# Attention on one core: the weights of four steps summed in two buffers, one of them in the place of four residual tiles

## The reference

```python
q, k = rope(q), rope(k)                     # each 16 x 2048 x 32
scores = q @ k.T / sqrt(32), causal
attn = softmax(scores)                      # over the keys
y = attn @ v
x = x + y.reshape(2048, 512) @ w_o
x = x + moe(rmsnorm(x, g2))
```

## Time and profile before

| | us |
|---|---|
| median of the runs | 2267.21 (2264.42 to 2269.95, 3 runs) |
| profiled execution, own time | 2257.79 |
| profiled execution, span | 2256.0 |
| attention stage in it | from about 965 to about 1709 |
| quad 1, from its first values to those of quad 2 | 1183.32 to 1341.37 |
| PE busy in the whole | 2048.9 (91%) |
| DVE, ACT, POOL busy | 1564.4, 1078.8, 581.5 |

### The profile page before, as it was taken

One profiled execution on the slowest core, in us unless ns is written; L12 is line 12 of the kernel. 1 busy time (PEld: TensorE's weight loads), 2 busy tenths in 40 slices (PEclk: granted clock), 3 DMA queues, 4 the chain that ended last, 5 costly groups with the idle time before them and its releaser, 6 DMA issues. The chain is left out here.

```text
span 2256.0 us, 42226 instructions
## 1 busy us (share of the span) xinstructions
PE 2048.9 (91%) x17716; PEld 1208.6 (54%) x17716; DVE 1564.4 (69%) x2563; ACT 1078.8 (48%) x1060; POOL 581.5 (26%) x447
## 2 busy tenths in 40 slices
PE   6899999999995899989999999999991599999997
PEld 3554444444442444544444444444440599999997
DVE  7789999999985666758777778778357544444442
ACT  6688898988980323213444444444330223332331
POOL 3410000000002012223454555545330222222211
PEclk9999999999998999959999999999995699999999
DMA  7321221212215013333013031010212444444421
GB/s 279 135 84 50 75 69 53 78 50 70 74 34 199 28 47 115 125 97 89 20 40 74 20 83 30 20 38 15 75 44 111 159 122 121 122 122 122 119 64 24
DMA packets 90905, 185.87 MB, mean 82 GB/s; under 512 B 14332, under 2 KB 23548, under 8 KB 86332
## 3 DMA queue, kind: packets, MB, share of 16 engines
q1 hardware_dynamic: 81756, 162.20, 22.0%
q0 software_dynamic: 8960, 20.98, 5.0%
HBM read 138.47 MB, written 40.23 MB: 79 GB/s over the span
## 5 line engine op out<-in xcount | busy, mean ns | idle before, releaser
L1515 DVE TENSOR_REDUCE t_rm<-t_m 128x1 f32<-128x512 f32 (+3 forms) x640 | 372.9, 606 | 148.5 <-PE t_m L1664 94.8
L1449 ACT ACTIVATE t_E<-t_s 128x1024 f32<-128x1024 f32 (+3 forms) x320 | 277.4, 895 | 410.9 <-PE t_s L1681 222.5
L1411 POOL TENSOR_TENSOR t_total<-t_E 128x1024 f32<-128x1024 f32 (+2 forms) x151 | 292.3, 1947 | 219.9 <-PE t_d L1708 214.1
L615 ACT ACTIVATE m_step<-m_ub,gat_bias 128x2048 bf16<-128x2048 f32 x128 | 250.0, 1989 | 13.9 <-DMA m_ub<-scratch_uac 8.5
L757 PE MATMUL m_bd<-m_mask,m_S 128*32 128x512 bf16 x3072 | 230.3, 379 | 11.0 <-DVE m_mask L705 11.0
L757 PE MATMUL m_bd<-gat_adjT,m_S 128*32 128x512 bf16 x2496 | 201.4, 379 | 4.8 <-PE m_dn L757 4.8
L757 PE MATMUL m_bd<-m_mask,m_neg 128*32 128x512 bf16 x2496 | 189.0, 379 | 0.0
L2038 POOL DMA_INDIRECT out<-e_ye,e_token x40 | 81.0, 2024 | 338.8 <-DVE e_ye L2141 334.1
L2202 PE MATMUL e_h<-e_xTh,e_w1h 128*128 128x320 f32 x512 | 159.0, 310 | 1.4 <-DVE e_xTl L2122 1.4
L2202 PE MATMUL e_h<-e_xTl,e_w1h 128*128 128x320 f32 x512 | 158.8, 310 | 0.0
L2202 PE MATMUL e_h<-e_xTh,e_w1l 128*128 128x320 f32 x512 | 158.8, 310 | 0.0
(11 more groups left out here) (362 smaller groups left out, 4084.6 us busy)
## 6 DMA issues: line engine op xcount, KB each, us to landing
a_adj<-in_adj SPq DMA_DIRECT2D x16, 1024.0 KB, 4.9
m_ub<-scratch_uac SPq DMA_DIRECT2D x16, 1024.0 KB, 5.1
e_w1r<-in_L_ffn_w SPq DMA_DIRECT2D x8, 2048.0 KB
e_w2r<-in_L_ffn_w SPq DMA_DIRECT2D x8, 2048.0 KB, 9.2
tq_Q<-scratch_parts SPq DMA_DIRECT2D x36, 256.0 KB, 4.6
gat_scale<-scratch_uac SPq DMA_DIRECT2D x32, 256.0 KB
scratch_parts<-o_hi SPq DMA_DIRECT2D x32, 256.0 KB, 2.2
scratch_parts<-o_lo SPq DMA_DIRECT2D x32, 256.0 KB, 2.7
```

Of the source, the lines that this page charges most:

```text
L615: act.activation(step(n), ub[h % 2][:, :].rearrange("p (t q) -> p t q", t=T), ACT.Relu, bias=bias[:, j, h:h + 1], scale=BIG).then_inc(step ...
L1411: pool.tensor_tensor(total[:, two, off:BANK], E[a % 3][:, two, off:BANK], E[(a + 1) % 3][:, two, off:BANK], ALU.add).then_inc(summed[z], 1)
L1449: act.activation(E[n % 3][:, two, off:BANK], ps_s[:, two, off:BANK], ACT.Exp, scale=SCALE).then_inc(exp_done[z], 1)
L1515: dve.tensor_reduce(rm[:, h, t, ch:ch + 1], ps_m[i % 2][:, 0:w], AX, ALU.max).then_inc(entry_read, 1)
```

## The change

Four steps in a row make one sum, in place of two. The first two are added from their `E` buffers, the third and fourth are each added to the sum in place. PE multiplies every sum of four by the ones once, at full width (512 columns), in the step n with n % 4 == 1, for the four steps that end at n - 2. There are two buffers of sums, used in turn, so that POOL waits only for the denominators of two sums before. The first buffer is the place of the residual tiles 12 to 15 in `X1`: SP stores these to a scratch in HBM at the head of the stage, ahead of the first loads, and loads them back behind the 39th of the 40 denominators, ahead of `load_grow`. In the last quad DVE takes the `z` = 1 half of the sums from step 145 on; all else stays on POOL.

```diff
+    FOUR = 4
+    SUMS = []
+    for n in range(QUADS * NS):
+        first_pair = 2 if STEPS[n % NS - n % FOUR + 1][2] else 1
+        SUMS.append((SUMS[-1] if n else 0) + (first_pair, 0, 1, 1)[n % FOUR])
...
-    BY_VECTOR = [k for k in range(QUADS * NS // 2) if 2 * k >= (QUADS - 1) * NS + HALF + 1]
+    BY_VECTOR = range((QUADS - 1) * NS + HALF + FOUR, QUADS * NS)
+    LAST_BY_VECTOR = []
...
-        total = st.sb("total", [P, G, BANK])
+        own_total = st.sb("total", [P, G, BANK])
+        away = slice(EARLY, T)
+        total = [X1[:, away, :], own_total]
...
+        def add_step(eng, n, z):
+            off, two, k = STEPS[n % NS][2], slice(2 * z, 2 * z + 2), n // FOUR
+            goal = total[k % 2]
+            eng.wait_ge(exp_done[z], n + 1)
+            if n % FOUR == 1:
+                if k == 0:
+                    eng.wait_ge(x_away, 16)
+                if k >= 1:
+                    eng.wait_ge(summed[z], SUMS[n - 2])
+                if k >= 2:
+                    eng.wait_ge(den_done, k - 1)
+                if off:
+                    eng.tensor_copy(goal[:, two, 0:off], E[(n - 1) % 3][:, two, 0:off]).then_inc(summed[z], 1)
+                first = E[(n - 1) % 3]
+            else:
+                eng.wait_ge(summed[z], SUMS[n - 1])
+                first = goal
+            eng.tensor_tensor(goal[:, two, off:BANK], first[:, two, off:BANK],
+                              E[n % 3][:, two, off:BANK], ALU.add).then_inc(summed[z], 1)
...
+                sp.dma_start(away_dram, X1[:, away, :]).then_inc(x_away, 16)
                 load_q(0, 1)
                 load_k_first(1)
...
                 load_o(2)
+                sp.wait_ge(den_done, QUADS * NS // FOUR - 1)
+                sp.dma_start(X1[:, away, :], away_dram).then_inc(x_back, 16)
                 load_grow()
...
                 def add_row(t):
+                    if t == EARLY:
+                        pool.wait_ge(x_back, 16)
...
-                for k in range(QUADS * NS // 2):
...
-                    if a >= (QUADS - 1) * NS:
-                        while added < EARLY and STEP_OF[added] < a % NS - 1:
+                for n in range(QUADS * NS):
+                    if n % FOUR:
+                        for z in range(1 if n in BY_VECTOR or n in LAST_BY_VECTOR else 2):
+                            add_step(pool, n, z)
+                    if n >= (QUADS - 1) * NS:
+                        while added < EARLY and STEP_OF[added] < n % NS - 2:
...
-                act.wait_ge(den_done, (q * NS + END[c] + 1) // 2)
+                act.wait_ge(den_done, (q * NS + END[c] + 1) // FOUR)
...
-                            act.wait_ge(summed[z], SUMS[(n - 3) // 2 + 1])
+                            act.wait_ge(summed[z], SUMS[n - 3])
...
-                        mm = pe.matmul(ps_d[h * DH:(h + 1) * DH, off:BANK], ones[:, :], total[:, h, off:BANK],
-                                       start=(kt == 0), stop=last)
+                        mm = pe.matmul(ps_d[h * DH:(h + 1) * DH, :], ones[:, :], total[k % 2][:, h, :],
+                                       start=(kt == 0), stop=(kt == 4 * c))
...
-                        if n >= 2 and n % 2 == 0:
-                            denominators(n // 2 - 1)
+                        if n > FOUR and n % FOUR == 1:
+                            denominators(n // FOUR - 1)
```

More of the change, by code:

```diff
@@ L1193, in stage_attention @@
     START = 28
-    SUMS = [0]
-    for k in range(QUADS * NS // 2):
-        SUMS.append(SUMS[k] + (2 if STEPS[2 * k % NS][2] < STEPS[(2 * k + 1) % NS][2] else 1))
+    FOUR = 4
[3 more added lines that the diff above has]
+        SUMS.append((SUMS[-1] if n else 0) + (first_pair, 0, 1, 1)[n % FOUR])
     EARLY = 12
@@ L1278, in stage_attention @@
         inverted, normed = sem("t_inverted"), sem("t_normed")
+        x_away, x_back = sem("t_x_away"), sem("t_x_back")
+        away_dram = z_dram.rearrange("(t p) d -> p t d", p=P)[:, away, :]
+        def add_step(eng, n, z):
[17 more added lines that the diff above has]
+                              E[n % 3][:, two, off:BANK], ALU.add).then_inc(summed[z], 1)
         with nc.Block() as block:
@@ L1338, in load_grow @@
                     for z in range(2):
-                        sp.wait_ge(summed[z], SUMS[FREE // 2])
+                        sp.wait_ge(summed[z], SUMS[FREE - 1])
                     sp.dma_start(grow, g2.partition_broadcast(P)).then_inc(grow_in, 16)
+                sp.dma_start(away_dram, X1[:, away, :]).then_inc(x_away, 16)
                 load_q(0, 1)
@@ L1523, in rows_of @@
                 def rows_of(t):
+                    if t == EARLY:
+                        dve.wait_ge(x_back, 16)
                     lk(dve.tensor_scalar(row(t), X1[:, t, :], mv[:, t, 0:1], rstd[:, t:t + 1],
@@ L1568, in finish @@
                     dve.scalar_tensor_tensor(row(t), row(t), rms[:, t:t + 1], grow, ALU.mult, ALU.mult).then_inc(z_ready, 1)
[L1570 to L1579, removed]
                 own, coming, turn = START, 0, []
@@ L1600, in _ @@
                             divide(*turn.pop(0))
-                        if s % 2 and (q * NS + s) // 2 in BY_VECTOR:
-                            pair_sum((q * NS + s) // 2)
+                        if q * NS + s - 1 in LAST_BY_VECTOR:
+                            add_step(dve, q * NS + s - 1, 1)
+                        if s % FOUR and q * NS + s in BY_VECTOR:
+                            add_step(dve, q * NS + s, 1)
                         while turn and q == QUADS - 1 and s > HALF:
@@ L1699, in denominators @@
                 def denominators(k):
-                    q, s = divmod(2 * k, NS)
+                    q, s = divmod(FOUR * k, NS)
                     c, kt, off = STEPS[s]
-                    last = kt == 4 * c + 2
                     if kt == 0 and k:
@@ L1705, in denominators @@
                     for z in range(2):
-                        pe.wait_ge(summed[z], SUMS[k + 1])
+                        pe.wait_ge(summed[z], SUMS[FOUR * k + 3])
                     for h in range(G):
-                        mm = pe.matmul(ps_d[h * DH:(h + 1) * DH, off:BANK], ones[:, :], total[:, h, off:BANK],
-                                       start=(kt == 0), stop=last)
+                        mm = pe.matmul(ps_d[h * DH:(h + 1) * DH, :], ones[:, :], total[k % 2][:, h, :],
+                                       start=(kt == 0), stop=(kt == 4 * c))
                     mm.then_inc(den_done, 1)
@@ L1784, in _ @@
                     own, coming = coming, 0
-                denominators(QUADS * NS // 2 - 1)
+                denominators(QUADS * NS // FOUR - 1)
                 for job in RJOBS[RPLACE[("share", 2)]:]:
```

## The result

| | before | after |
|---|---|---|
| median of the runs, us | 2266.97 (2264.42 to 2269.95, 4 runs) | 2296.73 (2291.7 to 2300.24, 4 runs) |
| ratio after to before | | 1.0129, 95% interval 1.0104 to 1.0154 |
| span of the profiled execution, us | 2256.0 | 2290.0 |
| mean granted clock of PE in it, share of 2.4 GHz | 0.956 | 0.942 |

The change makes the kernel 1.3% slower, outside the predicted range.

A forecast was written before the change was run, and what follows sets the result against it. PE was taken as the bound. Quads -1.0, +0.4, +1.6 and -3.1, end +1.4, head +1 and clock +1 made +1.3 us, carried to the median 2267.2: forecast 2268 us, range 2252 to 2283.

The forecast's parts named there:

- PE's saving: Fewer sets of denominators on PE: 7.2 us per quad, 28.7 us in all, if PE stays the bound everywhere.
- the clock's term: More PE stalls may bring more stretches at 1.2 GHz: between 0 and 6 us, taken as 1.
- The negation: DVE's negation of the maxima: three of four per quad blocked about 1.2 us by adds, half absorbed; 1.0 us per quad.
- The multiplications' wait: DVE's multiplications of the division wait for POOL's adds: mean 1.0 us, bounds 0.18 to 2.5.
- Steps 12 to 15: A group of quad 1 without divisions, set by POOL's six adds: 14.2 us, 1.2 us gained.
- the queue behind POOL's waits: Late sums from POOL holding up PE or ACT: costed at nothing, with some 3 us of slack.
- Step 21 on: Last quad from step 21, PE the bound: fewer denominators save 3.1 us.
- the end: Last denominators wait longer for POOL's wider add and run at full width: +1.4 us with handovers.
- the head: The 1 MB store ahead of six loads may delay them: cost between 0 and 3 us, taken as 1.
- DVE becomes the bound: Slower rival: multiplications wait 1.6 us each, +11 to +17 us, near 2281 with low clock; decided near 1.3 us; chance 0.35.
- PE keeps its gain: Faster rival: waits are absorbed where DVE has room, or multiplications fall in POOL's pauses; -14 us, 2254; chance 0.28.
- My two signs for slower: In the quads, PE or ACT waiting for POOL's sums would show the prediction wrong on the slow side.

The follow-up runs named there:

- a_neg: The changed kernel with the negation of the maxima done by the copy out of PSUM, its SBUF instruction removed; 2265.21 us, ratio 1.0010 to the kernel before.
- a_split: The changed kernel with each add cut into two of one head each; 2261.91 us, ratio 0.9987 to the kernel before.
- a_both: The changed kernel with the negation in the PSUM copy and the first 15 chunks' multiplications on GpSimd; 2227.19 us, ratio 0.9836 to the kernel before.
- b_both: The kernel before with the negation in the PSUM copy and the first 15 chunks' multiplications on GpSimd; 2266.16 us, ratio 1.0009.
- b_away: The kernel before with only the store of residual tiles 12 to 15 at the head and their load at the end; 2263.77 us, ratio 0.9996.
- a_mul: The changed kernel with the multiplications of the first 15 chunks moved from VectorE to GpSimd; 2279.14 us, ratio 1.0067 to the kernel before.

## Why the prediction was wrong

Most of its mechanism held, and PE's saving came. The step that failed is the clock's term of the sum. Without it my sum says +0.3 us, which is some 29 us of new idle time against 28.7 saved; PE's gaps grew by 27.0. The clock's term was 1 and measured about 31, which is all of the miss. That the idle time came out right in total is in part luck, for its terms were off in both directions.

- **The clock, the step that failed.** "Between 0 and 6 us; I take 1." The time at 1.2 GHz grew by 61.5 us, worth about 31: 13.7 us of it at the head of the stage, worth 7, and 47.8 behind it, worth 24. I took the clock for a small thing of its own; here stalls of PE can bring it, and a stall of 1.8 us was followed by 3.4 us of lost clock (step 33). With the negation's waits taken away (a_neg), 37.6 us of the time at 1.2 GHz go, and with shorter waits (a_split) 17.1. The clock's term should have been built from the number of stalls that the waits make.
- **The negation, mis-sized too.** "Off the bound half of that is absorbed; I count 1.0 us per quad". Its waits were near the forecast, 13.4 us over sixteen instances, three blocked per quad. But a_neg shows that they are worth 27 us, or some 8 for each of the three and a half quads with entries: 11.0 us of gaps and, at half of 37.6, 18.8 of clock. Little was absorbed. In quad 1 three pairs of steps behind blocked negations (20 and 21, 24 and 25, 32 and 33) are 2.9, 1.8 and 3.9 us longer than before, 8.6 in all, with one set of denominators in each pair before and after. The other 34 steps should have become 7.2 us shorter, as they hold PE's whole saving, and are 0.8 us longer; there the multiplications are blocked.
- **The multiplications' wait.** Forecast 1.0 us for each of 56, measured 46.0 us in all, 0.82 each: rightly sized, a little too high. Steps 16 to 19 of quad 1 took 1277.04 - 1257.43 = 19.6, forecast 19.0. Steps 12 to 15 took 1257.43 - 1241.64 = 15.8, forecast 14.2. The forecast has a slip: such a group loses one set of denominators, not two, so PE needs 15.35 - 0.89 = 14.46, more than POOL's 14.2, and the gain is 0.9 and not 1.2. a_both, with nothing blocked, took 14.5. Put right, this makes the sum some 3 us higher. The rest of the 15.8: a multiplication was blocked for 1.94 us at 1242.35 and the clock was low around it, as the values at 1241.64 (1.94 us) show.
- **PE's saving.** 40 sets of denominators, most of them 0.88 us from start to start: as forecast, but seven of them stood in stretches of 1.2 GHz and took 1.71. From b_both to a_both the saving comes through.
- **POOL.** Forecast about 120 us busy in quad 1, measured 117.4, its waits for denominators gone. No instruction of PE and no exponential waited for its sums inside the quads. "I cost the queue behind POOL's waits at nothing" held.
- **Step 21 on, the end, the head.** From the values of step 21 of the last quad to the last ones it went from 89.2 to 85.1 us, forecast -3.1; from those of step 19, behind which a negation is blocked, only from 97.0 to 95.0. PE's last wait for a sum grew from 1.60 to 2.65, within the +1.4. At the head PE waited 1.81 us for a load at 978.01, and the first values came 0.9 us later than before; I took 1. b_away confirms that the store costs nothing beyond it.
- **The rivals.** "DVE becomes the bound" had the sign right and the mechanism of the waits, but its point of decision, a mean wait of 1.3 us, was never reached: the loss came at 0.8. "PE keeps its gain" was to be told by a mean of L1487 below 0.8 us; it was 1.0. My two signs for slower, PE or ACT waiting for POOL's sums, did not appear, and the kernel was slower all the same.

The rule that I weighed in the negation's term (the Trainium skill, "SBUF — State Buffer", Who interferes with whom: the second to come is blocked for a whole instruction) is borne out by the 2.23 us of the negation and by a_split. The wait of 5.5 us in a_mul goes beyond it; there the measurement decides. I had excluded such a wait because of one copy at the end; one instance was too little for that.

Three smaller places of the working do not hold. "0.79 us of waiting made 0.86 us of step" compares two steps with two reciprocals to two steps with one, so it does not show by itself that the wait came through. The negation's term is 1.0 us in each quad, so without it the sum is more than 3 us lower, not "some 2". And the rival "PE keeps its gain" comes to -12 us by its own numbers, not -14.

Not settled: why short stalls bring the lower clock in some places and not in others, and why the stretch at the head is longer (64.9 to 71.7 us for 51.2) in every kernel with sums of four. The store, the negation and the multiplications are ruled out as the cause; nothing else was tried.

## What to carry to other kernels

Before work is added to GpSimd next to a VectorE that paces TensorE, list every VectorE instruction that works in SBUF alone, small ones too (here the multiplications, the negation and a scaling of rows were blocked, the reciprocals were not), and ask for each which TensorE instruction stands behind it: the smallest one here (16 columns) cost as much as all that the change gained. Price such a wait by the stall it makes and the clock that TensorE loses after it, not by the wait. Cures in order of cost: let an instruction that reads PSUM do the work (a_neg), cut GpSimd's instructions shorter (a_split), or give the blocked work to GpSimd itself, but only together with the first (a_both); then a change that lost 1.3% gains 1.6%.

## What the runs showed of the hardware

- GpSimd does not always give the port up between two instructions. In the kernel after all blocked instructions of VectorE ended with the add in which they had started or, if they started at the boundary of two adds, with the second. In a_mul six negations waited through three or more further instructions of GpSimd in a row, 3.9 to 5.5 us in all. What decides this is open.
- A third kind was blocked too, where it cost little: the `tensor_scalar` of 128 x 512 in SBUF (L1552) in the last quad, 0.54 us when free, up to 2.59 in the kernel after. The multiplication by -1 in the copy out of PSUM (a_neg, a_both) took 0.22 to 0.28 us in all of its 32 instances, as long as the plain copy did.
- The reciprocals (0.94 us each) and the reductions out of PSUM (606 ns before, 603 after) took as long in the kernel after as before, beside 42% more GpSimd time in quad 1.
- A TensorE stall of 1.8 us was followed by 6.8 us at 1.2 GHz (1329.8 to 1336.6 in the kernel after), though PE was busy for 8.2 of the 10.1 us from 1326.9.
- An add of 128 x 1024 on GpSimd took 2.36 us, two of 128 x 512 took 2.52 (four in a row in a_split 5.04): splitting cost 7%.
